# A token tower on one core: near and last embedding rows in one table, gathered once per item

## The chip, the cores and the metric

The kernel runs on one core of one Trainium2 chip. The metric is the device time of one execution in microseconds. Engines: PE (TensorE), DVE (VectorE), ACT (ScalarE), POOL (GpSimd) and SP (SyncE), each with its own instruction stream; they are ordered by semaphores only. POOL, ACT and SP also start DMA transfers, which 16 DMA engines carry out.

## What is computed

Token ids `x` are 16 sequences of 256, 4096 tokens, with values from 0 to 12563; the vocabulary is 50257 and the width 256. The embedding weight is stored by columns, `W` is 256 x 50257, so an embedding row is a column of it:

```python
h = jnp.take(L0_tok_W.T, x, axis=0)                    # 16 x 256 tokens x 256
h = h + attn(_layernorm(h))                            # 6 layers of linear attention
h = h + ffn(_layernorm(h))                             # 8 experts, top 2 of them, and a shared one
```

The change touches only the first line. What follows it: each of the six attention layers normalises, projects to q, k and v, takes softmax of q over the tokens and of k over the width, multiplies out `context`, projects and adds; the last part routes each token to two of eight experts.

## The kernel before

**Table stage.** Tokens are 32 tiles (`NT`) of 128; two tiles (`TB`) are one sequence, and an item of the attention stage is one layer of one sequence, 96 items in all. The columns of `W` are turned into rows chunk by chunk. A chunk is 512 columns (`VCH`); five chunks (`VBUF`) are a step of 2560 vocabulary rows (`VSTEP`). For a chunk, SP loads 512 KB (L381) into the buffer `VW[j]`, PE transposes it with eight matmuls against the identity (L783) into two PSUM banks, ACT copies one (L1037) and DVE the other (L1265) into `VR[j]`, and ACT stores `VR[j]` to a table in DRAM (L1039). SP's next load into `VW[j]` waits for the transposes, the next copy into `VR[j]` waits for the previous store of the same `j` (`s_wst[j]`), and PE waits for the copies of the banks that it writes again (`s_wcp`). Everything that follows in the loop of a step is ordered by these.

**Two tables.** The highest id decides how many steps are needed. The last four steps (`VLAST`) always go to `emb_last` (10240 rows, `VROWS`). The steps before them, `passes` in number, go one after the other to the same `emb_near` (2560 rows). With ids up to 12563 there is one pass, so five steps and 25 chunks in all: 5 stores to `emb_near`, 20 to `emb_last`. In the first step of `emb_last` ACT and DVE also convert the first layer's weights between the chunks (`cut`, L1046, L1050, L1278).

**Gathers.** When the near table's stores have landed, POOL gathers each of the 32 tiles from it with an indirect DMA (L580, `gather`): 128 rows of 1 KB by an index per partition. An index out of bounds is skipped and leaves its row in SBUF as it was. Then POOL takes 2560 off every index; an index that was in the near table becomes negative and gets `FAR` (2^20) added, so that it is out of bounds from now on. After the fill of both tables (`s_wst[j]` at `n + VLAST + 1` times 16) POOL gathers from `emb_last` item by item (`gather_item`), two tiles at a time, into the same tiles of `G`: what the near gathers found stays. ACT's store of a new pass waits until POOL is through with the near table (`s_reuse`).

**Item stage.** `gather_item(0)` is followed by `bn_stats` on DVE (L1388), the variance and root on POOL (L668 to L671), the normalisation on DVE (L1313), gamma and beta on POOL (L638, L642), high and low halves, a DMA transpose on SP (L441) and the projections on PE (L803). Later items' gathers stand on POOL between these.

`Wall` is one SBUF tensor, used as fp32 under the name `Wf`: the chunk buffers, `ident`, the ids, and, from its end backwards, the gathered tiles `G`. The weights of the experts overwrite it later. At the start POOL writes constants (L557 to L574) and then waits for the ids (`s_idx`).

Of the kernel before, what the change touches and what calls it, by code (L numbers as in the profile page):

```python
# [14 lines left out]
P = 128  # L15


def tower(nc, x_ids, tok_w, w_qkv, w_out, b_out, gamma, beta, gate_w, ew1, ew2, ew3, sw1, sw2, sw3, out):
    f32, f16, i32 = mybir.dt.float32, mybir.dt.float16, mybir.dt.int32
    ALU = mybir.AluOpType  # L20
# [4 lines left out]
    D, VOCAB = tok_w.shape  # L25
# [3 lines left out]
    NT = TOK // P  # L29
# [3 lines left out]
    NE = E + 1  # L33
# [23 lines left out]
    VSTEP = VCH * VBUF  # L57
    VBLK = VCH // P
    EXP = KH * 2 * HID + HC * D
# [4 lines left out]
    VROWS = VLAST * VSTEP  # L64
    FAR = 1 << 20
# [4 lines left out]
        v, last = step * VSTEP + j * VCH, VOCAB - VCH  # L70
        return eng.snap(v - (v > last) * (v - last)).with_bounds(min_val=0, max_val=last, guaranteed_mod_val=0, out_of_modulus=1)

    emb_near = nc.dram_tensor("emb_near", (VSTEP, D), f32, kind="Internal").ap()
    emb_last = nc.dram_tensor("emb_last", (VROWS, D), f32, kind="Internal").ap()
    slot_x = nc.dram_tensor("slot_x", (E * CAP + W2, ROW), f32, kind="Internal").ap()
    out_rows = out.rearrange("b s d -> (b s) d")
    h0_rows = nc.dram_tensor("h0_rows", (TOK, D), f32, kind="Internal").ap()
# [7 lines left out]
    with ctx:  # L85
        def sb(name, shape, dt, where=ctx):
            return where.enter_context(nc.sbuf_tensor(name, shape, dt))

        def sem(name):
            return ctx.enter_context(nc.semaphore(name))  # L90
# [3 lines left out]
        Wall = sb("Wall", [P, NE * 2 * EXP], f16)  # L94
        before = sb("before", [P, P], f16)
        ones16 = sb("ones16", [P, P], f16)
        idx = sb("idx", [P, NT], i32)
        epst = sb("epst", [P, TB], f32)
        mhalf = sb("mhalf", [P, NT], f32)
        stats = sb("stats", [P, 8, 6], f32)  # L100
        mv = sb("mv", [P, NT, 2], f32)
        rstd = sb("rstd", [P, NT], f32)
        far, idx_in = sb("far", [P, NT], i32), sb("idx_in", [P, NT], i32)
        h0b = sb("h0b", [P, 2, 4, D], f32)
        gw = sb("gw", [P, KH, E], f32)
        gwp = sb("gwp", [P, 2, KH, E], f16)
# [18 lines left out]
        s_wst = [sem(f"s_wst{i}") for i in range(VBUF)]  # L125
        s_xload = sem("s_xload")
        s_xhi, s_xlo = sem("s_xhi"), sem("s_xlo")
        s_gath = [sem(f"s_gath{i}") for i in range(4)]
        s_item = [sem(f"s_item{i}") for i in range(4)]
        s_fill = sem("s_fill")  # L130
        s_h0st, s_far = sem("s_h0st"), sem("s_far")
        s_reuse = sem("s_reuse")
# [4 lines left out]
        Wf = Wall[:, :].bitcast(f32)  # L137
# [3 lines left out]
        IDS = 2 * VBUF * VN + TOK + P + 512  # L141
        ids_rows, ids_f = Wf[0:NT, IDS:IDS + P].bitcast(i32), Wf[0:NT, IDS + P:IDS + 2 * P]
        row_max = Wf[0:NT, IDS + 2 * P:IDS + 2 * P + 1]
        ident = Wf[:, 2 * VBUF * VN + TOK:2 * VBUF * VN + TOK + P]
        G = Wf[:, NE * EXP - NT * D:].rearrange("p (t d) -> p t d", t=NT)


# [136 lines left out]
        def passes(eng):  # L284

            eng.wait_ge(s_idmax, 2)
            past_last = eng.value_load(idover[0:1, 0:1], min_val=0, max_val=VOCAB - 1 - VLAST * VSTEP)
            return eng.snap(past_last // VSTEP + 1)
# [267 lines left out]
        def _(pool):  # L556
# [16 lines left out]
            pool.wait_ge(s_padz, 1)  # L573
            pool.iota(padt[:, D:D + 1].bitcast(i32), pattern=[[0, 1]], base=TOK, channel_multiplier=1).then_inc(s_padt, 1)  # L574
            pool.wait_ge(s_idx, 1)
            pool.sem_inc(s_reuse, 1)

            def gather(t, ids, rows_, sem_):

                pool.indirect_dma_start(out=G[:, t, :], out_offset=None, in_=rows_,  # L580
                                        in_offset=bass.IndirectOffsetOnAxis(ap=ids[:, t:t + 1], axis=0),
                                        bounds_check=rows_.shape[0] - 1, oob_is_err=False).then_inc(sem_, 16)

            n = passes(pool)
            with pool.Fori(0, n) as q:
                for j in range(VBUF):
                    pool.wait_ge(s_wst[j], (q + 2) * 16)
                pool.sem_inc(s_passed, 1)
                pool.tensor_copy(idx[:, :], idx_in[:, :]).then_inc(s_far, 1)
                pool.wait_ge(s_far, q * 3 + 1)  # L590
                pool.sem_inc(s_passed, 1)
                for t in range(NT):
                    gather(t, idx, emb_near, s_gath[t % 4])
                pool.tensor_scalar(far[:, :], idx[:, :], VSTEP, FAR, ALU.is_lt, ALU.mult)
                pool.tensor_scalar(idx_in[:, :], idx[:, :], -VSTEP, None, ALU.add).then_inc(s_far, 1)
                pool.wait_ge(s_far, q * 3 + 2)
                pool.sem_inc(s_passed, 1)
                pool.tensor_tensor(idx_in[:, :], idx_in[:, :], far[:, :], ALU.add).then_inc(s_far, 1)
                pool.wait_ge(s_far, q * 3 + 3)
                pool.sem_inc(s_passed, 1)  # L600
                for g in range(4):
                    pool.wait_ge(s_gath[g], (q + 1) * (16 * NT // 4))
                pool.sem_inc(s_passed, 1)
                pool.sem_inc(s_reuse, 1)
            for j in range(VBUF):
                pool.wait_ge(s_wst[j], (n + VLAST + 1) * 16)
# [2 lines left out]
            def gather_item(i):  # L609

                if i >= 4:
                    pool.wait_ge(s_item[i % 4], 16 * TB * (i // 4))
                for t in range(TB * i, TB * (i + 1)):
                    gather(t, idx_in, emb_last, s_item[i % 4])

            def cut(n):

# [133 lines left out]
            for j in range(PAIRS):  # L751
# [5 lines left out]
                for w in range(2):  # L757
                    pool.indirect_dma_start(out=out_rows, out_offset=bass.IndirectOffsetOnAxis(ap=got(j % PAYS, w, 0, i32), axis=0),  # L758
                                            in_=yout[j % 2][:, w, :], in_offset=None, compute_op=ALU.add,
# [265 lines left out]
        def _(act):  # L1025
# [24 lines left out]
                A((Wc if isinstance(l, int) and l == 0 else Wn)[:, 0, at], Wsc[:, :], ACT.Copy).then_inc(s_wnhi, 1)  # L1050

            with act.Fori(0, m) as step:
                act.wait_ge(s_reuse, step + 1)
                for j in range(VBUF):
                    chunk(step, j, emb_near, j * VCH)
            for f_ in range(VLAST):
# [555 lines left out]
```

## Time and profile before

| | |
|---|---|
| median of 3 runs | 1443.81 us (1441.55 to 1447.90) |
| the profiled execution | 1445.67 us, span 1443.9 us |
| granted TensorE clock, mean | 0.95 |
| PE busy | 1268.4 us, 88% |
| DVE, ACT, POOL busy | 1031.5, 841.1, 963.1 us |
| DMA traffic | 156.66 MB, mean 108 GB/s |
| table stage | 0 to 106.57 us of the span |

How to read it: busy times are of one profiled execution on its one core; times within it count from the start of the span. "DMA share" is the mean busy share of the 16 DMA engines (rounding lets it pass 1). ACTq and SPq are the sequencers of ACT and SP, which issue DMAs. In a timeline row the first number is the start, the second the duration, and the bracket tells how long the engine had been idle and what ended that; "remote" there is a release that the profile ties to no engine and no transfer.

### The profile page before, as it was taken

To read this page: it belongs to the slowest core of one execution; us is meant where nothing else is said; L and a number is where in the kernel's file an instruction comes from. 1 tells how busy PE (TensorE), PEld (TensorE's weight loads), DVE (VectorE), ACT (ScalarE), POOL (GpSimd) and SP (SyncE) were. 2 spreads that over 40 slices of the span, in tenths; PEclk is the share of its full clock that TensorE was granted. 3 is DMA by queue.
4 is the path that set the end of the run, shared out by engine and by line. 5 is a ranking of instruction groups with operands and counts; after the bars stand their busy time and mean duration, and the time that the engine had idled before them with its cause. 6 is when DMAs were issued, how large, how long until landed. Compare 5 with 4: busy or idle time off the path is not lost. (4 is left out here: it accounts for less than half of the span.)

```text
span 1443.9 us, 36933 instructions
## 1 busy us (share of the span) xinstructions
PE 1268.4 (88%) x10994; PEld 1058.4 (73%) x10995; DVE 1031.5 (71%) x2647; ACT 841.1 (58%) x2302; POOL 963.1 (67%) x970
## 2 busy tenths in 40 slices
PE   3231798999999999999999999878998999999996
PEld 3221677888888888788888888744554888888885
DVE  2125799999999999999988889766555455545553
ACT  3110677788878878888887777666542233332321
POOL 0728778789888888898898889647652143343433
PEclk8565899999999999999999999998999999999998
DMA  9762555655564455335433445744434344544441
GB/s 337 237 233 57 113 143 134 160 122 126 129 139 88 118 124 119 64 66 116 79 65 66 105 95 97 112 70 123 128 104 145 57 67 59 73 62 68 63 64 14
DMA packets 350563, 156.66 MB, mean 108 GB/s; under 512 B 280714, under 2 KB 334713, under 8 KB 350496
## 3 DMA queue, kind: packets, MB, share of 16 engines
q1 hardware_dynamic: 315168, 116.92, 36.4%
q0 software_dynamic: 21600, 25.34, 10.3%
q10 hardware_dynamic: 13728, 13.63, 2.7%
q8 instruction: 26, 0.43, 0.1%
q14 instruction: 41, 0.34, 0.1%
HBM read 48.68 MB, written 43.16 MB: 64 GB/s over the span
## 5 line engine op out<-in xcount | busy, mean ns | idle before, releaser
L803 PE MATMUL bank<-hT,Wc 128*128 128x256 f16 x2304 | 285.8, 274 | 45.6 <-DMA hT<-hhl 31.8
L803 PEld LDWEIGHTS bank<-hT,Wc 128*128 128x128 f16 x2304 | 226.7, 98 | 73.3 <-issue 46.0
L758 POOL DMA_INDIRECT out_rows<-h0b,payin x78 | 121.4, 1557 | 209.8 <-DVE h0b L1577 178.1
L900 PE MATMUL bank<-xTg,Wall 128*128 128x256 f16 x1872 | 211.0, 273 | 0.0
L900 PEld LDWEIGHTS bank<-xTg,Wall 128*128 x1872 | 182.9, 98 | 21.8 <-issue 0.2
L1177 ACT ACTIVATE silu<-bank 128x512 f32<-128x512 f32 x110 | 65.6, 596 | 187.2 <-PE bank L900 145.0
L652 POOL TENSOR_TENSOR h0b<-h0b,rows 128x512 f32<-128x512 f32 x80 | 101.5, 1269 | 79.7 <-DVE h0b L1318 40.1
L803 PE MATMUL bank<-Wc,MT 128*128 128x256 f16 x1152 | 142.7, 274 | 13.4 <-DVE MT L1359 12.4
L1505 DVE SCALAR_TENSOR_TENSOR gT<-bank,silu 128x512 f32<-128x512 f32 x110 | 76.1, 691 | 105.5 <-ACT silu L1177 94.8
L803 PE MATMUL bank<-khl,eqT 128*128 128x256 f16 x1152 | 141.3, 272 | 5.5 <-DVE khl L1371 0.3
L803 PE MATMUL bank<-Wc,hT 128*128 128x256 f16 x1152 | 142.8, 274 | 0.0
L803 PEld LDWEIGHTS bank<-Wc,MT 128*128 128x128 f16 x1152 | 112.5, 98 | 29.6 <-issue 11.2
L803 PEld LDWEIGHTS bank<-khl,eqT 128*128 128x128 f16 x1152 | 109.5, 98 | 28.4 <-issue 16.0
L803 PEld LDWEIGHTS bank<-Wc,hT 128*128 128x128 f16 x1152 | 113.6, 99 | 13.8
L630 POOL TENSOR_TENSOR hhl<-h0b,hhl 128x512 f16<-128x512 f32 x96 | 112.1, 1168 | 0.5 <-ACT hhl L1130 0.3
L1117 ACT ACTIVATE MT<-bank,rzq 128x256 f16<-128x256 f32 x192 | 80.4, 470 | 54.8 <-PE bank L803 54.8
L916 PE MATMUL bank<-Wall,gThl 128*128 x936 | 108.8, 273 | 0.3 <-DVE gThl L1511 0.3
L847 PE MATMUL bank<-PR,vT 128*128 128x256 f16 x768 | 99.5, 272 | 8.0 <-ACT PR L1154 7.7
L931 PE MATMUL bank<-xT,Wall 128*128 128x512 f16 x384 | 96.3, 407 | 9.1 <-DVE gT L1505 8.4
L657 POOL TENSOR_TENSOR hhl<-h0b,rows 128x512 f16<-128x512 f32 x80 | 101.9, 1273 | 0.0
L653 POOL TENSOR_TENSOR X<-X,rows (+2 forms) x80 | 101.8, 1273 | 0.0
L658 POOL TENSOR_TENSOR h0b<-h0b,rows 128x512 f32<-128x512 f32 x80 | 101.8, 1273 | 0.0
(170 smaller groups left out, 2674.1 us busy)
## 6 DMA issues: line engine op xcount, KB each, us to landing
Wall<-in_L_tok_W SPq DMA_DIRECT2D x25, 512.0 KB
Wall<-in_L_ffn_ew SPq DMA_DIRECT2D x24, 512.0 KB, 4.1
emb_last<-Wall ACTq DMA_DIRECT2D x20, 512.0 KB
Wc<-Wn SPq DMA_DIRECT2D x40, 128.0 KB, 2.2
Wst<-in_L_attn_w_qkv SPq DMA_DIRECT2D x12, 384.0 KB
h_rows<-Wall SPq DMA_DIRECT2D x8, 512.0 KB
X<-h_rows POOLq DMA_DIRECT2D x8, 512.0 KB, 6.8
out_rows<-X SPq DMA_DIRECT2D x8, 512.0 KB
```

The source lines that it names most:

```text
L630: pool.tensor_tensor(hhl[q][:, 1, :, :], hf[:, :, :], hhl[q][:, 0, :, :], ALU.subtract).then_inc(s_h, 1)
L652: pool.tensor_tensor(xn[:, :, :], xn[:, :, :], row(0), ALU.mult).then_inc(s_hg, 1)
L653: pool.tensor_tensor(tiles(u), tiles(u), row(2), ALU.add).then_inc(s_xb, 1)
L657: pool.tensor_tensor(hhl[1 - p][:, 0, :, :], xn[:, :, :], row(1), ALU.add)
L658: pool.tensor_tensor(hf[:, :, :], xn[:, :, :], row(1), ALU.add).then_inc(s_hf, 1)
L758: pool.indirect_dma_start(out=out_rows, out_offset=bass.IndirectOffsetOnAxis(ap=got(j % PAYS, w, 0, i32), axis=0), in_=yout[j % 2][:, w, : ...
L803: last = mm(to, lhs(a, k, o), moving, start=(i == 0 and k == 0), stop=(i == 2 and k == 1))
L847: mm(o_ps[:, o, :], vT[p][:, a, k, blk(o)], PR[:, 0, k, :], start=(o == 0 and a == 0 and k == 0), stop=False)
L900: last = mm(to, cols(a, e, 2 * k + w, (2 * half + c) * P, P), moving, start=(n_ == 0), stop=(n_ == 5))
L916: last = mm(pb[4 + p][:, w * D:(w + 1) * D], gThl[:, p, a, c, w * P:(w + 1) * P], cols(b, e, KH * 2 + c // 2, c % 2 * D, D), start=(n_ == ...
L931: last = mm(pb[2 * (c % 2) + w][:, :].rearrange("p (t n) -> p t n", t=GT), cols(a, E, 2 * k + w, c * P, P), xT[g % RING][:, :, b, k, :], s ...
L1117: last = A(MT[:, 0, k, :], m_ps[:, k, :], ACT.Copy, scale=rzq[p][:, k:k + 1])
```

## The change

There is one DRAM table, `emb`, of 12800 rows: `emb_near` is its first 2560, `emb_last` the rest. The item gathers read the whole of it with the index as it stands after `n - 1` reductions, so the near rows of the last pass are found in the same gather as the last rows. Near gathers of their own are left for the passes whose near rows are overwritten by the next pass. They run in a loop of one tile per iteration: 33 iterations (`NT + 1`) per overwritten pass, and one iteration more at the end. An iteration clears a tile `found`, copies a column of indices to `now`, gathers into `found`, reduces the column, and adds `found` to the tile of `Gp`. `Gp` is `G` with one tile more in front, for column 0, whose indices are all `FAR`; it is cleared before the loop. `n` is 1 for this input, so the loop runs once, on column 0. ACT's wait for `s_reuse` counts 33 per pass, and its first increment stands behind the clearing of `Gp`.

```diff
--- before.py
+++ after.py
@@ -70,8 +70,8 @@
         v, last = step * VSTEP + j * VCH, VOCAB - VCH
         return eng.snap(v - (v > last) * (v - last)).with_bounds(min_val=0, max_val=last, guaranteed_mod_val=0, out_of_modulus=1)
 
-    emb_near = nc.dram_tensor("emb_near", (VSTEP, D), f32, kind="Internal").ap()
-    emb_last = nc.dram_tensor("emb_last", (VROWS, D), f32, kind="Internal").ap()
+    emb = nc.dram_tensor("emb", (VSTEP + VROWS, D), f32, kind="Internal").ap()
+    emb_near, emb_last = emb[0:VSTEP, :], emb[VSTEP:, :]
     slot_x = nc.dram_tensor("slot_x", (E * CAP + W2, ROW), f32, kind="Internal").ap()
     out_rows = out.rearrange("b s d -> (b s) d")
     h0_rows = nc.dram_tensor("h0_rows", (TOK, D), f32, kind="Internal").ap()
@@ -94,13 +94,13 @@
         Wall = sb("Wall", [P, NE * 2 * EXP], f16)
         before = sb("before", [P, P], f16)
         ones16 = sb("ones16", [P, P], f16)
-        idx = sb("idx", [P, NT], i32)
+        idx = sb("idx", [P, NT + 1], i32)
         epst = sb("epst", [P, TB], f32)
         mhalf = sb("mhalf", [P, NT], f32)
         stats = sb("stats", [P, 8, 6], f32)
         mv = sb("mv", [P, NT, 2], f32)
         rstd = sb("rstd", [P, NT], f32)
-        far, idx_in = sb("far", [P, NT], i32), sb("idx_in", [P, NT], i32)
+        far, idx_in = sb("far", [P, 1], i32), sb("idx_in", [P, NT], i32)
         h0b = sb("h0b", [P, 2, 4, D], f32)
         gw = sb("gw", [P, KH, E], f32)
         gwp = sb("gwp", [P, 2, KH, E], f16)
@@ -125,7 +125,7 @@
         s_wst = [sem(f"s_wst{i}") for i in range(VBUF)]
         s_xload = sem("s_xload")
         s_xhi, s_xlo = sem("s_xhi"), sem("s_xlo")
-        s_gath = [sem(f"s_gath{i}") for i in range(4)]
+        s_gath = sem("s_gath")
         s_item = [sem(f"s_item{i}") for i in range(4)]
         s_fill = sem("s_fill")
         s_h0st, s_far = sem("s_h0st"), sem("s_far")
@@ -142,6 +142,9 @@
         ids_rows, ids_f = Wf[0:NT, IDS:IDS + P].bitcast(i32), Wf[0:NT, IDS + P:IDS + 2 * P]
         row_max = Wf[0:NT, IDS + 2 * P:IDS + 2 * P + 1]
         ident = Wf[:, 2 * VBUF * VN + TOK:2 * VBUF * VN + TOK + P]
+        found = Wf[:, IDS + 3 * P:IDS + 3 * P + D]
+        now, zero = (Wf[:, IDS + 3 * P + D + c:IDS + 3 * P + D + c + n_].bitcast(i32) for c, n_ in ((0, 2), (2, 1)))
+        Gp = Wf[:, NE * EXP - (NT + 1) * D:]
         G = Wf[:, NE * EXP - NT * D:].rearrange("p (t d) -> p t d", t=NT)
 
 
@@ -573,6 +576,9 @@
             pool.wait_ge(s_padz, 1)
             pool.iota(padt[:, D:D + 1].bitcast(i32), pattern=[[0, 1]], base=TOK, channel_multiplier=1).then_inc(s_padt, 1)
             pool.wait_ge(s_idx, 1)
+            pool.memset(idx[:, 0:1], FAR)
+            pool.memset(zero[:, :], 0)
+            pool.memset(Gp, 0.0).then_inc(s_far, 1)
             pool.sem_inc(s_reuse, 1)
 
             def gather(t, ids, rows_, sem_):
@@ -581,26 +587,34 @@
                                         in_offset=bass.IndirectOffsetOnAxis(ap=ids[:, t:t + 1], axis=0),
                                         bounds_check=rows_.shape[0] - 1, oob_is_err=False).then_inc(sem_, 16)
 
+            ids = idx[:, 1:]
             n = passes(pool)
-            with pool.Fori(0, n) as q:
+            pool.tensor_copy(idx[:, 1:], idx_in[:, :]).then_inc(s_far, 1)
+            pool.wait_ge(s_far, 2)
+            with pool.Fori(0, (n - 1) * (NT + 1) + 1) as g:
+                q, t = pool.snap(g // (NT + 1)), pool.snap(g % (NT + 1))
                 for j in range(VBUF):
                     pool.wait_ge(s_wst[j], (q + 2) * 16)
                 pool.sem_inc(s_passed, 1)
-                pool.tensor_copy(idx[:, :], idx_in[:, :]).then_inc(s_far, 1)
-                pool.wait_ge(s_far, q * 3 + 1)
+                col, tile = idx[:, bass.ds(t, 1)], Gp[:, bass.ds(t * D, D)]
+                pool.memset(found[:, :], 0.0)
+                pool.tensor_tensor(now[:, 0:1], col, zero[:, :], ALU.add).then_inc(s_far, 1)
+                pool.wait_ge(s_far, g * 5 + 3)
                 pool.sem_inc(s_passed, 1)
-                for t in range(NT):
-                    gather(t, idx, emb_near, s_gath[t % 4])
-                pool.tensor_scalar(far[:, :], idx[:, :], VSTEP, FAR, ALU.is_lt, ALU.mult)
-                pool.tensor_scalar(idx_in[:, :], idx[:, :], -VSTEP, None, ALU.add).then_inc(s_far, 1)
-                pool.wait_ge(s_far, q * 3 + 2)
+                pool.indirect_dma_start(out=found[:, :], out_offset=None, in_=emb_near,
+                                        in_offset=bass.IndirectOffsetOnAxis(ap=now[:, 0:1], axis=0),
+                                        bounds_check=VSTEP - 1, oob_is_err=False).then_inc(s_gath, 16)
+                pool.tensor_scalar(far[:, :], now[:, 0:1], VSTEP, FAR, ALU.is_lt, ALU.mult).then_inc(s_far, 1)
+                pool.wait_ge(s_far, g * 5 + 4)
                 pool.sem_inc(s_passed, 1)
-                pool.tensor_tensor(idx_in[:, :], idx_in[:, :], far[:, :], ALU.add).then_inc(s_far, 1)
-                pool.wait_ge(s_far, q * 3 + 3)
+                pool.tensor_scalar(now[:, 1:2], now[:, 0:1], -VSTEP, None, ALU.add).then_inc(s_far, 1)
+                pool.wait_ge(s_far, g * 5 + 5)
                 pool.sem_inc(s_passed, 1)
-                for g in range(4):
-                    pool.wait_ge(s_gath[g], (q + 1) * (16 * NT // 4))
+                pool.tensor_tensor(col, now[:, 1:2], far[:, :], ALU.add).then_inc(s_far, 1)
+                pool.wait_ge(s_gath, g * 16 + 16)
                 pool.sem_inc(s_passed, 1)
+                pool.tensor_tensor(tile, tile, found[:, :], ALU.add).then_inc(s_far, 1)
+                pool.wait_ge(s_far, g * 5 + 7)
                 pool.sem_inc(s_reuse, 1)
             for j in range(VBUF):
                 pool.wait_ge(s_wst[j], (n + VLAST + 1) * 16)
@@ -611,7 +625,7 @@
                 if i >= 4:
                     pool.wait_ge(s_item[i % 4], 16 * TB * (i // 4))
                 for t in range(TB * i, TB * (i + 1)):
-                    gather(t, idx_in, emb_last, s_item[i % 4])
+                    gather(t, ids, emb, s_item[i % 4])
 
             def cut(n):
 
@@ -1050,7 +1064,7 @@
                 A((Wc if isinstance(l, int) and l == 0 else Wn)[:, 0, at], Wsc[:, :], ACT.Copy).then_inc(s_wnhi, 1)
 
             with act.Fori(0, m) as step:
-                act.wait_ge(s_reuse, step + 1)
+                act.wait_ge(s_reuse, step * (NT + 1) + 1)
                 for j in range(VBUF):
                     chunk(step, j, emb_near, j * VCH)
             for f_ in range(VLAST):
```

## Rows read from the trace of the kernel before

**Rows 1.** The page: DMA share in tenths and rate, 40 slices of 36.1 us.

```profile
DMA  9762555655564455335433445744434344544441
...
GB/s 337 237 233 57 113 143 134 160 122 126 129 139 88 118 124 119 64 66 116 79 65 66 105 95 97 112 70 123 128 104 145 57 67 59 73 62 68 63 64 14
```

**Rows 2.** Stretches: length, busy us (and instructions) by engine, PEclk, DMA share, GB/s.

```profile
0.00:10.00 10.00, 5.08 (x31) 4.95 (x33) 2.95 (x8) 2.09 (x3) 2.89 (x16) 1.00 0.79 266
...
20.00:36.00 16.00, 7.18 (x40) 5.77 (x40) 4.20 (x9) 6.77 (x16) 0.21 (x1) 0.71 1.07 400
...
36.00:56.00 20.00, 7.05 (x40) 6.81 (x40) 4.38 (x8) 4.22 (x9) 15.33 (x15) 0.67 0.99 326
...
56.00:83.00 27.00, 6.19 (x33) 5.96 (x34) 2.31 (x4) 1.79 (x3) 18.08 (x21) 0.56 0.35 96
...
83.00:105.00 22.00, 8.46 (x48) 7.83 (x47) 6.31 (x14) 5.59 (x10) 0.00 (x0) 0.66 1.04 358
...
105.00:107.00 2.00, 0.00 (x0) 0.00 (x0) 0.00 (x0) 0.00 (x0) 0.43 (x1) 0.50 0.02 5
```

**Rows 3.** Timeline of POOL: first and last near gather, first item gather.

```profile
36.40 1.24 POOL L580 DMA_INDIRECT Wall<-emb_near,idx  x1 [0.99 <-POOL idx L589]
...
77.33 1.01 POOL L580 DMA_INDIRECT Wall<-emb_near,idx  x1 [0.30 <-issue]
...
106.57 1.11 POOL L580 DMA_INDIRECT Wall<-emb_last,idx_in  x1 [26.98 <-issue]
```

**Rows 4.** Timeline of ACT: stores issued (ACTq) and copies that waited.

```profile
37.09 0.39 ACTq L1039 DMA_DIRECT2D emb_last<-Wall  x1
...
44.00 0.38 ACTq L1039 DMA_DIRECT2D emb_last<-Wall  x1
...
56.55 0.60 ACT L1037 ACTIVATE Wall<-bank 128x512 f32<-128x512 f32 x1 [6.49 <-remote]
...
82.07 0.60 ACT L1037 ACTIVATE Wall<-bank 128x512 f32<-128x512 f32 x1 [13.60 <-remote]
...
83.00 0.38 ACTq L1039 DMA_DIRECT2D emb_last<-Wall  x1
...
91.77 0.60 ACT L1037 ACTIVATE Wall<-bank 128x512 f32<-128x512 f32 x1 [2.30 <-DMA emb_last<-Wall]
...
99.68 0.61 ACTq L1039 DMA_DIRECT2D emb_last<-Wall  x1
```

**Rows 5.** DMA queues from 36 to 107 us: packets, MB, share of 16 engines.

```profile
q10 hardware_dynamic: 10292, 10.21, 40.7%
...
q1 hardware_dynamic: 3323, 5.87, 27.9%
...
q0 software_dynamic: 1536, 0.90, 5.0%
```

**Rows 6.** Timeline of the start, and one POOL operation on two tiles.

```profile
2.16 0.95 POOL L568 MEMSET h0b<- 128x1024 f32 x1
...
4.29 0.17 DVE L1246 CAST idx_in<-bank 128x32 int32<-128x32 f32 x1
...
7.39 1.28 ACT L1037 ACT_TABLE_LOAD   x1 [7.39 <-PE bank L783]
...
117.86 1.25 POOL L638 TENSOR_TENSOR h0b<-h0b,rows 128x512 f32<-128x512 f32 x1
```

**Rows 7.** Line L580, forms: ns min/median/max, first and last start; landing times.

```profile
L580 POOL DMA_INDIRECT Wall<-emb_near,idx x32: 1005/1009/1243, 36.4 to 77.3; - x32
...
L580 POOL DMA_INDIRECT Wall<-emb_last,idx_in x32: 994/1012/1151, 106.6 to 236.2; - x32
...
DMA to landing us min/median/max: 2.7/2.9/4.5
```

**Rows 8.** Timeline of DVE: first statistics of item 0.

```profile
110.79 0.75 DVE L1388 BATCH_NORM_STATS2 stats<-Wall 128x6 f32<-128x256 f32 x2 [9.57 <-DMA Wall<-emb_last,idx_in]
```

**Rows 9.** The page, DMA issues: count, KB each.

```profile
Wall<-in_L_tok_W SPq DMA_DIRECT2D x25, 512.0 KB
```

## Prediction

> **What bounds the kernel now.** The change touches only how the embedding rows are fetched, so I read the slices of the page first. The second slice (36 to 72 us) still moves 237 GB/s, but its DMA engines are less busy than in the first [rows 1]. I then cut the table stage into stretches [rows 2]. From 20 to 36 us the DMA engines are full (share 1.07, 400 GB/s); from 56 to 83 us they are not (0.35, 96 GB/s), and PE, DVE and ACT together work only 10 us of those 27; from 83 to 105 us they are full again (1.04, 358 GB/s). Nothing computes and nothing is transferred for much of 27 us, in a stage that is otherwise limited by transfers.
>
> What lies in the hole is seen on POOL's own timeline [rows 3]: the 32 gathers from the near table start at 36.40, one every 1.3 us, the last at 77.33 us. ACT's timeline shows what the hole is made of [rows 4]. A buffer of the table is copied again only when its previous store has landed. The store issued at 37.09 lets go at 56.55 (19.5 us), the one of 44.00 at 82.07 (38.1 us), and that second one only after the last gather. The store of 83.00, with no gather beside it and the engines full, lets go at 91.77 (8.8 us). So stores get slow as long as gathers are being issued, and recover within 4 us of the end of them. The gathers themselves moved 0.90 MB in 1536 packets, against 16.08 MB of loads and stores after 36 us [rows 5]: it is not their bytes.
>
> The stage ends at 106.57 us with the first gather of item 0 [rows 3], which waits until every store has landed. The item stage hangs on it: DVE's first statistics wait 9.57 us, until 110.79, for this gather's data [rows 8]. Everything behind it (1337 us of the span) starts from there, so I let a shift of 106.57 carry through whole. The time outside the span is 1445.67 - 1443.9 = 1.8 us, unchanged; the profiled execution is 1.9 us above the median 1443.81.
>
> **The change part by part.** The ids of this input stop at 12563, so there is one pass (one near step, four last steps).
>
> *The 32 near gathers go.* The new loop runs (1 - 1) x 33 + 1 = 1 time, and its one gather has FAR as index in all 128 partitions: it moves nothing. POOL loses 31 gathers, 31 x 1.3 = 40 us of its own time, which nobody waits for by itself. What counts is the hole. Without it the stage from 36 us is 16.08 MB of loads and stores [rows 5] at the rate of full engines. The bounds of that rate are 400 GB/s (20 to 36 us) and 358 GB/s (83 to 105 us) [rows 2]; I take the middle, 379 GB/s, because the rest of the stage is first loads and stores mixed, as in the one, and then stores alone, as at the end of the other. 16.08 / 0.379 = 42.4 us, so the last bytes arrive at 78.4 us. Before, the traffic had ended by 105 us (5 GB/s in the two microseconds behind it [rows 2]) and POOL's gather began at 106.57, so add 1.6: 80.0 us. Gain 26.6 us. By 400 GB/s it is 36 + 40.2 + 1.6 = 77.8, gain 28.8; by 358 it is 36 + 44.9 + 1.6 = 82.5, gain 24.1.
>
> Is anything else late next? The 40 transposes between 36 and 56 us, five chunks, kept PE busy 7.05 us [rows 2], 1.4 us a chunk; ten stores left ACT between 83.00 and 99.68 us [rows 4], 1.7 us a chunk and partly waiting; the transfer of one chunk, in and out, is 1.05 MB or 2.8 us. So PE, DVE and ACT cover themselves. The DMA queues could run dry for a moment at the turn of a step, since only five loads and five stores are ever open. The bound for this: the third step's copies begin at 43 us, just before the store of 44.00 [rows 4], the fourth's no sooner than one turn of 5 x 2.8 = 14 us later, the fifth's another turn later, at 71; then 7.9 us to the last store and 6.9 to the gather (99.68 - 91.77 and 106.57 - 99.68 [rows 3, 4]), 85.8 us, gain 20.8. This is the pessimistic end; work that is queued ahead makes the turns overlap, so I stay with the bytes.
>
> *The start.* POOL now clears 33 tiles, 128 x 8448 f32, before it lets ACT begin its first store of the near table. The MEMSET of 1024 elements took 0.95 us [rows 6], so this one takes 7.8 us. It starts with the ids at about 4.5 us (the cast at 4.29 [rows 6]) and ends at 12.3. ACT's first operation began at 7.39 [rows 6], so its first copies come 4.9 us later, if the increment of the semaphore waits for the MEMSET, and 0 if it does not. What hides this: DMA is what counts, and at 10 us much is open: by the code SP has issued nine chunk loads of 512 KB [rows 9], the first layer's weights and vectors (1.4 MB) and ACT the fill of 0.5 MB, 6.6 MB in all, of which 2.7 are moved (266 GB/s for 10 us [rows 2]); 3.9 MB are 10 us of work at 379 GB/s. ACT's stores join at about 14 us, before that runs out. I take 0, with 4.9 as the end of the range where the five copies gate everything. If POOL worked at the pace of its arithmetic (1.25 us for 512 elements [rows 6]) the clearing would take 21 us; a MEMSET is nearer to the MEMSET row.
>
> *The dummy iteration.* Behind the near stores, where the old gathers began (36.40 [rows 3]), POOL does a 256-wide clear, three or four small operations, one gather, an add of 128 x 256 (under 1.25 us [rows 6]) and waits for its landing (2.7 to 4.5 us where a landing is shown [rows 7]); with register work I estimate some 10 us, over by about 46 us. Behind it on POOL's queue stands only the wait for the last stores, at 80 us. Cover 34 us; without that cover it would cost its 10 us. Its gather can still slow the stores, as the old ones did: 1 of 32 gathers, so by the old loss (26.6 / 32) 0.8 us; between 0 and that, I take 0.
>
> *The item gathers* read one table at the raw index. Before, the near rows were out of bounds there (a fifth) and now none is. Issue cost did not depend on how many rows were skipped: median 1009 ns with four fifths skipped, 1012 ns with a fifth [rows 7]. Landing was 2.7 to 4.5, median 2.9 us [rows 7]; a fifth more rows moves this by tenths at most, for items 0 and 1 alone, where DVE waits. Nothing counted.
>
> A rule to weigh: DMA: Bandwidth & Descriptors, section "Queues, rings and completion order", of the Trainium skill says that each DMA engine takes turns between the queues that have work, one packet at a time. By it the gathers would take no more than their turns, and the rival "only their bytes" below follows. The trace disagrees on its face: share 0.35 and 96 GB/s while stores are open for 38 us. The same page, section "Latency and other measured facts", gives as a guess that some DMA engines are slow because the software-written descriptor rings load their ports; no row here shows single engines, but a mean share of 0.35 with stores open is what a few late engines would look like.
>
> **Sum.** -26.6 + 0 + 0 + 0: 1445.67 - 26.6 = 1419.1 on the profiled execution's own scale, 1443.81 - 26.6 = 1417.2 against the median. Range: best 1443.81 - 28.8 = 1415.0, worst 1443.81 - 20.8 + 4.9 = 1427.9; the three runs of before spread by 4 us up and 2 down, so 1412 to 1430.
>
> **Rivals.**
> 1. *The start is on the path.* The late first stores delay each step by 4.9 us because the copies of the second step need those stores landed. For: stores gate copies [rows 4]. Against: engines are full then, and loads come sooner if stores don't share with them. 1417.2 + 4.9 = 1422.1, inside the range.
> 2. *Only their bytes.* The hole is not the gathers' doing (a few late DMA engines, or loads of the vocabulary columns), and happens to end with them. Then only 0.90 MB goes, 0.90 / 0.379 = 2.4 us: 1441.4, or 1446 with the late start. For: the rule above, and 4 us between the last gather and the release at 82.07. Against: three changes of pace that coincide with gathers starting and stopping, and a full stretch before and behind [rows 2, 4].
> 3. *Slower.* The hole stays, and POOL's clearing runs at its arithmetic pace, 21 us, so that ACT begins at 25.5, 18 us late, past the 10 us of open loads. Of this 18 - 2.4 counts: 1459. It ends slower as soon as the release is later than the gain of 2.4 us and the cover together. For: nothing in the rows but that POOL's arithmetic is slow. Against: the MEMSET rows.
> 4. *One gather is enough.* The single all-skipped gather stops the stores nearly as the 32 did, for it has more skipped rows than any of them, and only half of the hole goes: 1443.81 - 13 = 1431. For: near gathers skip most rows, and the item gathers, which skip few, land in 2.9 us. Against: the slowdown grew over many gathers (19.5, then 38.1 us), as a backlog does.
>
> **How the numbers follow.** Forecast 0.74; rival 1 0.12; rival 2 0.06; rival 3 0.03; rival 4 0.05. The likeliest gives 1417. The range 1412 to 1430 holds the first two, 0.86 before I allow for what I have not thought of. A measurement of this kernel can tell about 0.5%, 7.2 us, from no change: faster is forecast, rivals 1 and 4 = 0.91; same is rival 2, 0.06; slower 0.03.
>
> **What would show it.** In the profile after: no stretch between 36 us and the end of the stage with a DMA share under about 0.9 for more than 2 or 3 us; ACT's waits for stores under 15 us each; the first item gather near 80 us (78 to 86); one MEMSET of 7 to 8 us on POOL from about 4.5; ACT's first copy at about 12; the 128x256 add before 50; everything from the first item gather to the end as long as before, 1337 us within 3. Wrong it is if the DMA share still falls to a third with no gather on POOL (rival 2), if ACT's second step's copies start later than 27 us (rival 1), if the hole sits right behind the one gather (rival 4), or if the item stage has grown.

## The result and the profile after

The changed kernel takes 1422.57 us (four runs, 1419.03 to 1424.57) against 1443.60 for the kernel before on the same chip (four runs, 1441.55 to 1447.90): ratio 0.9843, 95% interval 0.9823 to 0.9863, that is 20 to 26 us less. The profiled execution took 1419.03 us, with a span of 1417.3.

That is not the whole result. On another chip, with 12 runs of the changed kernel and 17 of the kernel before, they take 1412.73 and 1413.76 us: ratio 0.9991, interval 0.9983 to 1.0000. What the change removes is a cost that the kernel before pays on one chip or two, and not on three others. Each of these chips was visited once, so whether the cost belongs to the chip or to something that went on there at the time was not separated; where the text says that it depends on the chip, this is left open. The sections below show how that came out.

The page of the kernel after, DMA share in tenths and rate in 40 slices (here 35.4 us each), to be laid beside [rows 1]:

```profile
DMA  9944655745645563335343445654334444444441
...
GB/s 338 370 130 93 153 148 123 184 105 124 141 87 118 126 144 67 64 67 131 62 73 74 111 91 95 98 84 133 106 106 136 73 59 70 61 71 61 68 62 13
```

The third slice fell from 233 to 130 GB/s, since the table's traffic now ends within it. The stretches, with the columns of [rows 2] (length, busy us and instructions of PE, PE's loads, DVE, ACT and POOL, granted clock, DMA share, GB/s):

```profile
20.00:36.00 16.00, 7.72 (x40) 6.30 (x40) 4.23 (x9) 6.80 (x16) 0.46 (x2) 0.71 1.07 400
...
36.00:56.00 20.00, 11.86 (x65) 10.75 (x66) 7.11 (x12) 6.58 (x13) 2.71 (x5) 0.67 1.02 353
...
56.00:80.00 24.00, 9.63 (x56) 8.92 (x55) 6.13 (x13) 4.99 (x9) 0.00 (x0) 0.71 1.03 373
```

Between 56 and 80 us the share is 1.03, where it was 0.35. The granted clock is 0.67 and 0.71 of 2.4 GHz (0.67 and 0.56 before). From 56 to 80 us PE is busy 9.6 of 24 us, so little can hang on it there; from 43 to 46 us PE is busy all the time at a clock of 0.50, which the part on the table stage takes up. POOL's timeline (start, duration, line, operation, idle time and what ended it) has the clearing, the loop's one gather, its add, and the first item gather:

```profile
4.58 7.14 POOL L581 MEMSET Wall<- 128x8448 f32 x1
...
36.49 1.26 POOL L604 DMA_INDIRECT Wall<-emb,Wall  x1 [1.04 <-issue]
...
42.24 0.73 POOL L616 TENSOR_TENSOR Wall<-Wall 128x256 f32 x1 [3.30 <-DMA Wall<-emb,Wall]
...
81.33 1.13 POOL L586 DMA_INDIRECT Wall<-emb,idx  x1 [38.36 <-issue]
```

The first item gather comes at 81.33 us instead of 106.57 [rows 3], 25.2 us earlier. ACT begins at the same time as before [rows 6], and DVE's first statistics follow the gather by 4.30 us (4.22 before [rows 8]):

```profile
7.41 1.28 ACT L1051 ACT_TABLE_LOAD   x1 [7.41 <-PE bank L797]
```

```profile
85.63 0.75 DVE L1402 BATCH_NORM_STATS2 stats<-Wall 128x6 f32<-128x256 f32 x2 [9.34 <-DMA Wall<-emb,idx]
```

From the first item gather to the end of the span it is 1417.3 - 81.33 = 1336.0 us, before 1443.9 - 106.57 = 1337.3. So in the two traces 25.2 of the 26.6 us lie in the table stage. The medians differ by 21.0; the profiled execution is the fastest of its four.

### The profile page after: what moved, and what is told of

Same layout as the page of the kernel before. It is cut to its first block and busy times, and to the rows that moved or that the text cites. A ratio compares the mean times of both kernels' runs of the same rounds, so it can differ in the third digit from the quotient of the medians.

```text
span 1417.3 us, 36879 instructions
## 1 busy us (share of the span) xinstructions
PE 1271.3 (90%) x10994; PEld 1058.6 (75%) x10995; DVE 1028.6 (73%) x2647; ACT 840.5 (59%) x2302; POOL 940.5 (66%) x945
## 3 DMA queue, kind: packets, MB, share of 16 engines
q10 hardware_dynamic: 13728, 13.63, 2.7%
```

## Experiments: what makes the hole

Stage times below are the start of POOL's first item gather in the trace. Runs that are compared were made on one chip, with the kernel before timed beside them. The first four were made where the kernel before takes 1444.73 us, as on the chip of the result (whether it is the same one is not known).

**The near gathers put back** into the changed kernel, behind its loop. One run, 1448.56 us.

```diff
+            for t in range(NT):
+                gather(t, ids, emb_near, s_gath)
+            pool.wait_ge(s_gath, 16 + 16 * NT)
+            pool.sem_inc(s_passed, 1)
             for j in range(VBUF):
                 pool.wait_ge(s_wst[j], (n + VLAST + 1) * 16)
```

> The changed kernel with the 32 near gathers put back: after its one-column loop, POOL issues one gather per tile from the near table at the raw ids (four fifths of the indices out of bounds), as before; the item gathers overwrite what they find. Theory A (gathers that are being issued hold up ACT's stores): the hole in the DMA share comes back between 56 us and the end of the gathers near 85, the first item gather moves from 81.3 us back to 106 to 110, the time to about 1446. Theory B (the hole had another cause, the gathers cost their bytes): 0.9 MB more, first item gather at 84, time about 1425.

POOL's timeline, last near gather and first item gather:

```profile
84.47 1.00 POOL L586 DMA_INDIRECT Wall<-emb,idx  x1 [0.30 <-issue]
...
108.82 0.99 POOL L586 DMA_INDIRECT Wall<-emb,idx  x1 [23.36 <-DMA emb<-Wall]
```

The hole is back: 108.82 us against 81.33, and the time with it. Whether there is one table or two makes no difference; the gathers do. Theory B (their bytes) said 84 and falls on this chip.

**All indices out of bounds** (`alt` is a new tile of indices, and `gather` is told to use it): 1447.16 us.

```diff
+            pool.memset(alt[:, :], FAR).then_inc(s_alt, 1)
+            pool.wait_ge(s_alt, 1)
+            for t in range(NT):
+                gather(t, alt, emb_near, s_gath)
+            pool.wait_ge(s_gath, 16 + 16 * NT)
+            pool.sem_inc(s_passed, 1)
```

> The changed kernel with 32 more gathers from the near table behind its one-column loop, every index of them out of bounds, so that they move nothing. Theory A1 (it is the issuing of a gather, whatever it moves): first item gather at 106 or later, as with the near gathers. Theory A2 (it is the rows that are moved, small packets between large ones): no hole, first item gather at 81 to 83. If skipped rows are what makes it slow, later than with the raw ids, beyond 110.

```profile
84.77 1.00 POOL L587 DMA_INDIRECT Wall<-emb,alt  x1 [0.30 <-issue]
...
106.30 1.00 POOL L587 DMA_INDIRECT Wall<-emb,idx  x1 [20.53 <-DMA emb<-Wall]
```

**All indices in bounds**: 1449.14 us.

```diff
+            V.tensor_scalar(alt[:, :], idx_in[:, :], 2047, None, ALU.bitwise_and).then_inc(s_alt, 1)
...
+            pool.wait_ge(s_alt, 1)
+            for t in range(NT):
+                gather(t, alt, emb_near, s_gath)
+            pool.wait_ge(s_gath, 16 + 16 * NT)
+            pool.sem_inc(s_passed, 1)
```

> The changed kernel with 32 more gathers from the near table behind its one-column loop, every index of them in bounds (the id's low 11 bits, made on DVE at the start), 4.2 MB in all; the item gathers overwrite them. Theory A1 (issuing counts): the hole is there, first item gather at 106 plus up to 9 us for 3.3 MB more. Theory A2 (rows moved count): a hole up to five times that of the raw ids. Theory A3 (skipped rows count): only the bytes, 4.2 MB / 0.385 = 11 us: first item gather at 92.

```profile
87.27 1.00 POOL L587 DMA_INDIRECT Wall<-emb,alt  x1 [0.30 <-issue]
...
109.93 1.00 POOL L587 DMA_INDIRECT Wall<-emb,idx  x1 [21.66 <-DMA emb<-Wall]
```

No rows moved gives 106.30, a fifth of the rows 108.82, all rows 109.93. Neither rows moved nor rows skipped decide (A2 and A3 fall); the issuing does (A1). From no rows to all rows it is 3.6 us more. A gather that moves no row still leaves packets on POOL's queue. From 56 to 83 us the run with all rows skipped issued 21 gathers and has there

```profile
q0 software_dynamic: 1008, 0.01, 2.3%
```

48 packets for each, as many as the gathers of the kernel before had (1536 for 32 [rows 5]). So "issuing" stands for POOL's own work and these small packets together; the runs don't part them.

**POOL busy, no transfer**: 1427.60 us.

```diff
+            for k in range(6):
+                pool.memset(G[:, :, :], 0.0).then_inc(s_alt, 1)
+                pool.wait_ge(s_alt, k + 1)
```

> The changed kernel with POOL kept busy for about 42 us behind its one-column loop by six MEMSETs of the gathered tiles (128x8192 each, one after the other) and no transfer. Theory C (a busy POOL, its port to SBUF, holds up the others): first item gather well behind 81.3, up to 106. Theories A: no hole; POOL ends near 85 to 86 us, so the first item gather comes at about 86, 5 us late for that reason alone, with the last store landed at 79 to 80 as in the changed kernel.

```profile
43.23 41.85 POOL L621 MEMSET Wall<- 128x8192 f32 x6 [0.36 <-POOL Wall L617]
...
86.75 1.13 POOL L587 DMA_INDIRECT Wall<-emb,idx  x1 [1.68 <-issue]
```

```profile
56.00:83.00 27.00, 8.35 (x48) 7.88 (x48) 13.15 (x13) 5.00 (x9) 26.77 (x5) 0.72 0.91 326
```

POOL was through at 85.08 and gathered at 86.75; from 56 to 83 us the DMA rate was 326 GB/s, no hole. A POOL busy with MEMSETs holds up nobody here, and theory C falls. That the effect was there to be seen in this execution is shown by the scatters later in it, of which the next section tells: DVE's addition there has the same unnamed waits as in the other traces with the hole.

```profile
DVE X L1548 <- remote: 15.4, 4, 4.3
```

## What is late in the hole

The prediction read ACT's waits [rows 4] as stores that land late. The run with all rows skipped speaks against it. Its stretches show that from 70 to 78 us no engine but POOL works and nothing is moved:

```profile
56.00:83.00 27.00, 1.36 (x11) 0.89 (x9) 1.97 (x3) 1.68 (x3) 20.85 (x21) 0.60 0.50 150
...
70.00:78.00 8.00, 0.00 (x0) 0.00 (x0) 0.00 (x0) 0.00 (x0) 6.12 (x7) 0.50 0.02 0
```

and its queue of stores had by 71 us moved

```profile
q10 hardware_dynamic: 9504, 9.44, 37.6%
```

The page of before has 13728 packets on q10 (the queue of ACT's stores) for 26 stores (25 chunks and the fill), 528 each; 9504 is 18 times 528, and 18 is what ACT had issued. All stores were through, and still ACT's next copy came only at 78.45.

SP's queue in the kernel before settles whom they wait for. SP's load of a chunk waits for one thing alone, the increment `s_wtr[j]` that PE makes behind a chunk's last transpose. PE's timeline, ACT's copy of the fifth chunk, and SP's loads there:

```profile
40.98 7.05 PE L783 MATMUL bank<-Wall 128*128 128x128 f32 x40 [10.43 <-DVE Wall L1265]
...
68.62 6.01 PE L783 MATMUL bank<-Wall 128*128 128x128 f32 x32 [20.59 <-issue]
```

```profile
67.87 0.60 ACT L1037 ACTIVATE Wall<-bank 128x512 f32<-128x512 f32 x1 [10.72 <-remote]
```

```profile
49.60 0.37 SPq L381 DMA_DIRECT2D Wall<-in_L_tok_W  x1
...
56.87 0.38 SPq L381 DMA_DIRECT2D Wall<-in_L_tok_W  x1
...
68.16 0.37 SPq L381 DMA_DIRECT2D Wall<-in_L_tok_W  x1
...
82.13 0.93 SPq L381 DMA_DIRECT2D Wall<-in_L_tok_W  x2
```

PE had 40 transposes, five chunks, behind it at 48.03 us. The loads that wait for these five were issued at 43.13, 44.82, 49.60, 56.87 and 68.16, the last 20 us late. ACT's copies came at 49.47, 56.55 and 67.87, DVE's at the same times, and the next of all three at 82.07 to 82.13. Three engines are let go together, and what they have in common is PE's increment. So it is not a landing that is late: a wait on PE is. The run with all rows skipped agrees: there SP's queue has 38.1 us of unnamed waits between 36 and 92 us. The profile has no releaser for these waits and calls them remote. SP's waits from 36 to 90 us, before:

```profile
SPq L381 <- remote: 31.3, 4, 10.6
...
SPq L381 <- PE bank L783: 11.8, 2, 11.3
```

The same shows a second time, where POOL issues 64 scatters (L723, indirect transfers to DRAM) in the routing. In the kernel before PE's 24 products for one block end at 1028.93, DVE is free at 1028.76, its addition L1530, which waits for just them, starts at 1033.23, and POOL's run of scatters ends at 1031.62:

```profile
1026.15 2.78 PE L948 MATMUL bank<-Wall,gThl 128*128 128x256 f16 x24
```

```profile
1028.07 0.69 DVE L1505 SCALAR_TENSOR_TENSOR gT<-bank,silu 128x512 f32<-128x512 f32 x1
...
1033.23 0.69 DVE L1530 SCALAR_TENSOR_TENSOR X<-bank,X 128x512 f32<-128x512 f32 x1 [4.46 <-remote]
```

```profile
1030.66 0.96 POOL L723 DMA_INDIRECT slot_x<-xrow,sloti  x1 [0.30 <-issue]
```

## Experiments: it depends on the chip

The next runs fell on another chip, and there the kernel before took 1415.85 us.

**16 skipped gathers**, 1411.32 us on that chip; later again on a third one, 1415.72 (kernel before 1414.34).

```diff
+            pool.memset(alt[:, :], FAR).then_inc(s_alt, 1)
+            pool.wait_ge(s_alt, 1)
+            for t in range(16):
+                gather(t, alt, emb_near, s_gath)
+            pool.wait_ge(s_gath, 16 + 16 * 16)
+            pool.sem_inc(s_passed, 1)
```

> The changed kernel with 16 gathers (all indices out of bounds) behind its one-column loop instead of 32, back to back, about 44 to 65 us. Theory D (each gather adds a piece of delay, 32 of them 25 us): first item gather near 81.3 + 12.5 = 94. Theory E (a store that is open while gathers run is released only when they are over, or by chance; what is lost is what lies behind the time DMA would need without them): the stores lose from about 52 to 69 us, first item gather near 90 or a little above. If a backlog builds up first and 16 gathers are too few for it: 82 to 84.

> The changed kernel with 16 all-skipped gathers, on the same chip as the kernel before. If that one takes about 1414 us here: first item gather at 81, no loss, as on the other such chip. If it takes about 1445 us here: theory D (every gather adds its piece of 25 us / 32) says 94, theory E (stores are let go when the gathers are over, 65 us) says 85 to 90.

```profile
63.59 1.00 POOL L587 DMA_INDIRECT Wall<-emb,alt  x1 [0.30 <-issue]
...
81.06 1.00 POOL L587 DMA_INDIRECT Wall<-emb,idx  x1 [16.48 <-DMA emb<-Wall]
```

81.06 us, and 81.98 the second time: no loss. **The same 16, paced by MEMSETs** between them: 1424.32 us, first item gather at 92.55.

```diff
+            pool.memset(alt[:, :], FAR).then_inc(s_alt, 1)
+            pool.wait_ge(s_alt, 1)
+            for t in range(16):
+                gather(t, alt, emb_near, s_gath)
+                pool.memset(G[:, 16:21, :], 0.0).then_inc(s_alt, 1)
+                pool.wait_ge(s_alt, t + 2)
+            pool.wait_ge(s_gath, 16 + 16 * 16)
+            pool.sem_inc(s_passed, 1)
```

> The same 16 all-skipped gathers, each followed by a MEMSET of 128x1280 on POOL (about 1.2 us), so that they cover 42 us as the 32 did. Theory D (each gather adds its piece): as with 16 back to back. Theory E (any stretch of gathers holds the stores until it is over): first item gather at 106. Theory F (it is a queue that 1.3 us between gathers overfill and 2.6 us do not): no loss, first item gather at 87, which is when POOL itself is through.

ACT's last store was issued at 75.60, and POOL's last gather at 89.04, so only POOL itself was late. **32 plain transfers** from POOL's queue: 1420.90 us, first item gather at 91.31, about where the 11 us that were expected for their bytes put it.

```diff
+            for t in range(16):
+                pool.dma_start(G[:, t, :], emb_near[t * P:(t + 1) * P, :]).then_inc(s_gath, 16)
+            for t in range(16):
+                pool.dma_start(G[:, 16 + t, :], emb_near[t * P:(t + 1) * P, :]).then_inc(s_gath, 16)
+            pool.wait_ge(s_gath, 16 + 16 * NT)
+            pool.sem_inc(s_passed, 1)
```

> The changed kernel with 32 plain transfers of 128 KB from POOL's queue instead of gathers (near rows in order, no index), behind its one-column loop; the item gathers overwrite them. Theory G (any transfer that POOL issues holds up the release of the stores): first item gather above 100. Theory H (only indirect ones do): only the bytes, 4.2 MB / 0.385 = 11 us, first item gather near 92.

These three decide nothing between theories D to H. Where there is no hole to begin with they could not: on their chip the kernel before took 1415.85 us, and on the third chip, where its trace was taken again, it shows no hole.

**The kernel before again**, unchanged, on a third chip: 1415.54 us.

> The kernel before, unchanged, profiled again on another chip. So far chips fall in two kinds: where the gathers make a hole the kernel before took 1442 to 1448 us, elsewhere 1410 to 1416, and the changed kernel 1419 to 1425 there and 1409 to 1414 here. Theory K (the hole under the 32 gathers is a matter of the chip): with a time near 1445 this trace shows stores let go 19 to 38 us late, DMA share about 0.35 from 56 to 83 us, first item gather near 106; with a time near 1414 it shows the same 32 gathers with the DMA engines full from 36 us on and the first item gather at 80 to 83. Theory L (the gathers cost the same everywhere, the faster chips gain elsewhere): time near 1414 and first item gather near 106 all the same.

```profile
35.89 1.24 POOL L580 DMA_INDIRECT Wall<-emb_near,idx  x1 [1.01 <-POOL idx L589]
...
76.82 1.00 POOL L580 DMA_INDIRECT Wall<-emb_near,idx  x1 [0.30 <-issue]
...
84.69 1.10 POOL L580 DMA_INDIRECT Wall<-emb_last,idx_in  x1 [5.58 <-issue]
```

```profile
36.00:56.00 20.00, 10.37 (x64) 9.43 (x64) 7.32 (x12) 7.01 (x14) 15.43 (x16) 0.74 1.02 351
...
56.00:83.00 27.00, 9.58 (x56) 8.87 (x56) 6.15 (x13) 5.00 (x9) 17.92 (x20) 0.70 1.02 366
```

The same 32 gathers at the same pace, 35.89 to 76.82 us, beside full DMA engines (share 1.02), and the first item gather at 84.69 us, not 106.57 (the expectation had said 80 to 83). SP waits for PE and for no release without a name:

```profile
SPq L381 <- PE bank L783: 21.8, 10, 11.3
```

PE's five chunks lie as in the first trace, from 41.38 to 48.48 us, and here ACT's copy of the fifth comes at 49.48 us, 1.0 us after PE's end, where the first trace had 19.8 us:

```profile
41.38 7.10 PE L783 MATMUL bank<-Wall 128*128 128x128 f32 x40 [10.43 <-DVE Wall L1265]
```

```profile
49.48 0.60 ACT L1037 ACTIVATE Wall<-bank 128x512 f32<-128x512 f32 x1 [0.71 <-ACT Wall L1037]
```

So the waits differ, and PE's work, as the traces have it, does not. Theory K holds, with chip or occasion left open as said above, and L falls. All traces fall in line with it: the six from the chip of the result and the first four experiments have unnamed waits, and the eight from the three other chips have none at all. The scatters agree. The 64 of them, same count and same duration each, span 127.5 us in the first trace of before and 116.5 here:

```profile
L723 POOL DMA_INDIRECT slot_x<-xrow,sloti x64: 956/960/1439, 978.6 to 1106.1; - x64
```

```profile
L723 POOL DMA_INDIRECT slot_x<-xrow,sloti x64: 954/960/1446, 959.4 to 1075.9; - x64
```

DVE's addition behind PE's products has 15.3 us of unnamed waits in the one trace and none in the other. The changed kernel's two traces differ alike: 126.6 us on the chip of the result (952.6 to 1079.2), 116.5 on that of the next run (956.8 to 1073.3). The changed kernel is still 9.8 us slower on the chip of the result by its medians, and its scatters, which were left as they are, account for 10.1 us of the traces. The sum is not that clean: the two spans differ by 6.0 us only, since the stretch from the first item gather to the first scatter is 4.6 us shorter on the chip of the result. Why it is so was not looked into.

**The changed kernel again**, 12 runs, on a fourth chip: 1412.73 us, ratio 0.9991, first item gather at 80.91.

> The changed kernel once more, with five timed rounds, to size the gain: its trace put the first item gather 25.2 us earlier, the first four times 21 us. If the gain is what the table stage gives, the ratio is 0.982 to 0.983 (25 us); if something behind the table stage gives some of it back in most executions, 0.985.

Neither 0.982 nor 0.985: both expectations took the first chip for all. What is left there of the gain is 1.0 us (0 to 2.4). By the traces the table stage gives 84.69 - 80.91 = 3.8 us, of which 0.90 MB [rows 5] explain 2.4; but these are traces of two chips, and the rest of the two spans is 1329.1 and 1330.4, so 1.3 us go the other way.

**The clearing ahead of ACT**: 1414.37 us, on the chip of the first run with 16 gathers.

```diff
             pool.memset(Gp, 0.0).then_inc(s_far, 1)
+            pool.wait_ge(s_far, 1)
             pool.sem_inc(s_reuse, 1)
```

> The changed kernel with one wait more: POOL waits for its MEMSET of 33 tiles before it lets ACT begin (in the changed kernel the increment overtakes the MEMSET: ACT starts at 7.41 us while it runs to 11.72). Prediction's own claim (the late start is hidden by 10 us of open loads): ACT's first copy at 12 us, first item gather at 81.3 as before, within 1 us. Rival 1 (it is on the path): first item gather at 86.

```profile
11.97 1.28 ACT L1052 ACT_TABLE_LOAD   x1 [11.97 <-POOLq L583]
```

```profile
84.12 1.13 POOL L587 DMA_INDIRECT Wall<-emb,idx  x1 [38.85 <-issue]
```

ACT begins 4.6 us later, the first item gather comes at 84.12, 3.1 us behind the 81.06 of the run with 16 gathers on the same chip. The changed kernel's two traces and the two with 16 gathers have it between 80.91 and 81.98, so 2 to 3 us of the delay are on the path.

**No iteration for a single pass, and the weights' conversion spread** over two steps, five runs: 1408.93 us, ratio to the kernel before 0.9967 (0.9954 to 0.9980) on the fourth chip, 3.8 us under the changed kernel there.

```diff
-            with pool.Fori(0, (n - 1) * (NT + 1) + 1) as g:
+            with pool.Fori(0, (n - 1) * (NT + 1)) as g:
...
-                    if f_ == 0:
-                        for n_ in range(2 * j, min(2 * j + 2, WSL)):
-                            cut(n_, 0, n_)
+                    n_ = VBUF * f_ + j
+                    if n_ < WSL:
+                        cut(n_, 0, n_)
```

(DVE's half of the conversion is spread in the same way.)

> The changed kernel with the last iteration of its loop dropped, so that it runs 0 times for one pass, and with the first layer's weights converted one piece per chunk in two steps instead of two pieces per chunk in one. The dip of the DMA rate between 43 and 46 us (142 and 206 GB/s) comes from ACT and DVE being at one copy per 4 us there; with one piece per chunk a copy comes every 2.7 us, and the first item gather is 1 to 3 us earlier, 78.5 to 80.5. If the dip is due to the one gather at 36.5 us instead, the same. If neither matters, 81.3. Time 0 to 3 us under the changed kernel's.

```profile
78.76 1.13 POOL L586 DMA_INDIRECT Wall<-emb,idx  x1 [36.00 <-issue]
```

```profile
36.00:56.00 20.00, 12.71 (x67) 12.47 (x68) 7.97 (x14) 8.46 (x19) 2.69 (x5) 0.67 1.07 393
```

The rate from 36 to 56 us is 393 GB/s, where the changed kernel had 362 on this chip; the first item gather is 2.2 us earlier than the 80.91 of the changed kernel on this chip. The gather moved by what was expected (1 to 3 us), the time by a little more (0 to 3). Which of the two edits did it was not separated: the run changes both. The traces point at the conversion: in the changed kernel PE's five chunks wait for a copy until 40.50 us on this chip, here until 37.68, and the rate while the one gather was issued (36 to 40 us) is 389 GB/s with it and without. It is the fastest version here.

## Why the prediction was right, and where it was not

The time and the range held: 1417 forecast, 1422.57 measured, 1412 to 1430 stated. They held on the kind of chip whose trace the prediction had.

*The table stage.* First item gather forecast at 80.0, measured 81.33; gain 26.6 forecast, 25.2 measured. The terms: the mixed part ran faster than the 379 GB/s I took (395 to 402 in the stretches from 50 to 65 us), and against it stood a dip, 142 and 206 GB/s in two slices of 1.2 us at 43 to 46. The two partly cancel, which is luck. Where the dip lies, the step "PE, DVE and ACT cover themselves" was wrong: PE had waited 10.57 us for DVE's copy, which came late between the pieces of the weights' conversion, and then did its 40 transposes without a break, at a granted clock of 0.50, while the loads waited for it:

```profile
43.00:46.00 3.00, 3.00 (x16) 3.00 (x15) 1.38 (x2) 1.20 (x2) 0.00 (x0) 0.50 0.80 208
```

Three us at 208 instead of 379 GB/s are 1.4 us, and the stage ended 1.3 us after the forecast. On the fourth chip the dip is there too (222 GB/s) at a granted clock of 0.87, so the late start of the transposes is the greater part of it and not the clock. The bound of 85.8 for queues that run dry was too far out.

*The start.* Forecast a MEMSET of 7.8 us, measured 7.14. Forecast ACT at about 12 us, hidden at no cost; ACT began at 7.41, since POOL's plain semaphore increment doesn't wait for the MEMSET ahead of it. The term 0 was right for the case that I named second (no wait for the MEMSET). The step that was taken as its reason, 10 us of open loads that hide a late start, was wrong: with the wait put in, 2 to 3 of 4.6 us came through (and the trace of before has eight chunk loads issued by 10 us, not nine). Rival 1 was nearer to that case.

*The dummy iteration.* Over at 42.97 us (46 forecast); no hole behind it. Rival 4 (one skipped gather is enough) fell here, and the runs with 16, made where there was no hole, show nothing on it for this chip.

*The item gathers.* The median stayed where it was, 1014 ns with no row skipped:

```profile
L586 POOL DMA_INDIRECT Wall<-emb,idx x32: 994/1014/1147, 81.3 to 208.5; - x32
```

*The mechanism.* Half right. "Stores get slow as long as gathers are being issued" named the right cause and its timing; the runs with none, a fifth and all of the rows show that it is the issuing. The step that failed is "a buffer is copied again only when its previous store has landed", read as the only wait of the copy. The copy waits for PE's increment too, and SP, which waits for nothing else, was let go at the same moments. With SP's queue read, the late stores would not have been written.

*Rival 2, only their bytes*, had a chance of 0.06 at 1441.4, a gain of 2.4 us. Where I gave evidence against it, all of it came from one chip. On the fourth chip the gain is 1.0 us (0 to 2.4): there this rival is what came out, at another level of time, and the forecast of 26.6 us would have missed by 25.6. That the prediction was measured on the kind of chip that its trace came from is no merit of it. The rule from "DMA: Bandwidth & Descriptors", "Queues, rings and completion order", of the Trainium skill, that an engine takes turns between queues, was weighed as one that this trace refutes. The run of the kernel before on the third chip agrees with it (gathers and stores side by side at a share of 1.02), and the hole doesn't refute it either, for the transfers were not what was late.

Open: why these increments of PE come late, and why on some chips alone. Whether 16 gathers, spaced ones, or plain transfers from POOL do the same where the hole exists was not tried, nor which part of a gather's issue does it, POOL's work or its packets. Whether PE's last transposes themselves ended later than the trace has them cannot be told for certain, since the ends of matmuls are modelled; against it stands that the PE rows of the two kinds of trace are alike (7.05 and 7.10 us for 40).

## What to carry to other kernels

When several engines leave a wait in the same microsecond, look for the semaphore that they share, and read the queue that waits for it alone; the nearest transfer is a guess. A stall that the profile can't name ("remote" on a single core) should be looked at on a second chip before a change is built on it: here it is worth 21 us on one kind and 1 us on the other. Where a trace shows such waits beside a long run of indirect transfers issued by POOL, try that run outside the stage in which the others hand work to each other by PE's semaphores; where it shows none, there is little to gain.

## What the runs showed of the hardware

On the chip of the result and that of the first four experiments, waits on PE were let go as much as 20 us late while POOL issued a gather every 1.3 us, even when the gathers moved no rows; during 42 us of MEMSETs on POOL instead there was no delay. On one other chip the same 32 gathers caused no such delay, and on three others the same 64 scatters caused none (116.5 to 117.9 us, against 124.7 to 128.3). A semaphore increment that POOL executes as an instruction of its own passes a MEMSET of 7.14 us that is still running: ACT began at 7.41 us, the MEMSET ended at 11.72. A gather of 128 rows takes POOL the same 1.0 us whether all, four fifths, a fifth or none of its rows are skipped.
